# Two graph attention layers on one core: the keys are kept in block order of columns, and VectorE reads two operands through strides

## The reference

```python
def layer0(x, adj):                      # Wq, Wk, Wv, bv, Wo, bo
    q, k = heads(x @ Wq.T), heads(x @ Wk.T)
    v = heads(x @ Wv.T + bv)
    scores = einsum('bqhd,bkhd->bhqk', q, k) * 384**-0.5 + 2 * adj
    scores = where(any(scores != 0, -1), scores, -inf)
    return (softmax(scores) @ v) @ Wo.T + bo

def layer1(x, adj):                      # Wq, bq, Wk, bk, Wv, bv, beta
    q, k, v = heads(x @ Wq + bq), heads(x @ Wk + bk), heads(x @ Wv + bv)
    scores = q @ k.T / sqrt(32) + beta * adj
    scores = where(adj > 0, scores, -9e15)
    return softmax(scores) @ v

x = layernorm(x + layer0(x, adj))        # adj: (128, 128, 128), x: (128, 128, 384)
x = layernorm(x + layer1(x, adj))
```

## Time and profile before

| | before |
|---|---|
| median of 3 runs | 2470.41 us (2469.18 to 2474.57) |
| the profiled execution | 2472.7 us |
| its span, first to last instruction | 2470.9 us |
| TensorE busy | 2158.2 us, 87% |
| VectorE busy | 2100.6 us, 85% |
| ScalarE busy | 1764.0 us, 71% |
| GpSimd busy | 1235.6 us, 50% |
| mean granted TensorE clock | 0.974 |

### The profile page before, as it was taken

The page is one execution under the profiler, slowest core; times in us unless marked ns, Lnnn a source line. Parts: engine busy times, 40 slices in busy tenths (PEclk is TensorE's granted clock), DMA queues, the critical chain, the costliest instruction groups (busy, mean ns, idle before and its releaser), DMA issues.

```text
span 2470.9 us, 84478 instructions
## 1 busy us (share of the span) xinstructions
PE 2158.2 (87%) x23808; PEld 1941.3 (79%) x23808; DVE 2100.6 (85%) x8579; ACT 1764.0 (71%) x7432; POOL 1235.6 (50%) x1932
## 2 busy tenths in 40 slices
PE   5999988898989899889898888898988899889863
PEld 5888888788888788788788888888888888788753
DVE  4788888898888898888898888898888888888864
ACT  5577777777777777677777777777777777677653
POOL 3545555555545555455555555555554555455442
PEclk8999999999999999999999999999999999999976
DMA  4354544544544544454544544544544544454442
GB/s 139 78 131 117 136 127 114 136 124 119 130 121 115 135 126 112 127 131 115 134 126 115 134 125 116 134 124 116 133 124 120 130 124 112 126 131 116 101 116 74
DMA packets 234783, 300.42 MB, mean 122 GB/s; under 512 B 26704, under 2 KB 226384, under 8 KB 234576
## 3 DMA queue, kind: packets, MB, share of 16 engines
q1 hardware_dynamic: 234576, 298.43, 46.6%
HBM read 46.67 MB, written 25.17 MB: 29 GB/s over the span
## 4 chain that ended last, share of the span: by engine, by line
DVE 37%; issue 31%; PE 15%; ACT 11%; DVEq 2%; POOL 2%; ACTq 1%; DMA 1%; SPq 0%; POOLq 0%
DVE neg_s L680 12%; ACT prob L567 8%; DVE abs_max L729 5%; PE s_bank L410 5%; DVE stats L652 3%; DVE neg_max L680 3%; PE r_bank L360 3%; PE r_bank L362 2%; PE r_bank L361 2%; DVE x1T_lo L702 2%; DVE y L744 2%; DVE y L643 2%; PE r_bank L353 1%; DVE flip L696 1%; DVE v L755 1%
## 5 line engine op out<-in xcount | busy, mean ns | idle before, releaser
L567 ACT ACTIVATE prob<-neg_s,neg_max 128x128 f32<-128x128 f32 x3072 | 1186.4, 391 | 391.9 <-DVE neg_max L680 390.0
L680 DVE CUSTOM_DVE_ANT_0 neg_s<-s_bank,bias 128x128 f32<-128x128 f32 x3072 | 673.9, 287 | 184.5 <-PE s_bank L410 115.7
L567 ACT ACTIVATION_READ_ACCUMULATOR prob<-neg_s,neg_max 128x1 f32 x3072 | 587.5, 191 | 0.0
L915 POOL TENSOR_TENSOR prob<-prob,inv_sum 128x512 f32<-128x512 f32 x384 | 388.8, 1041 | 306.8 <-DVE inv_sum L766 306.8
L360 PE MATMUL r_bank<-x1T_hi,w_hi 128*128 128x256 f32 x1152 | 362.7, 315 | 2.7 <-ACT k0T L542 1.4
L907 POOL TENSOR_TENSOR y<-y,x_late 128x384 f32<-128x384 f32 x128 | 127.5, 996 | 474.5 <-DVE y L744 474.5
L360 PE MATMUL r_bank<-xT_hi,w_hi 128*128 128x256 f32 x1152 | 351.2, 305 | 9.5 <-DVE xT_lo L702 9.5
L361 PE MATMUL r_bank<-x1T_lo,w_hi 128*128 128x256 f32 x1152 | 330.1, 287 | 0.0
L362 PE MATMUL r_bank<-x1T_hi,w_lo 128*128 128x256 f32 x1152 | 329.1, 286 | 0.0
L362 PE MATMUL r_bank<-xT_hi,w_lo 128*128 128x256 f32 x1152 | 326.6, 284 | 0.0
L361 PE MATMUL r_bank<-xT_lo,w_hi 128*128 128x256 f32 x1152 | 326.3, 283 | 0.0
(11 more groups left out here) (73 smaller groups left out, 5196.2 us busy)
## 6 DMA issues: line engine op xcount, KB each, us to landing
prob0T<-flip SPq DMA_DIRECT2D x512, 192.0 KB, 3.6
prob1T<-stage SPq DMA_DIRECT2D x512, 192.0 KB, 3.8
x_in<-in_x_dram SPq DMA_DIRECT2D x128, 192.0 KB, 3.3
x_late<-x SPq DMA_DIRECT2D x64, 384.0 KB, 2.6
out_dram<-y SPq DMA_DIRECT2D x128, 192.0 KB, 2.3
adj<-in_adj_dram SPq DMA_DIRECT2D x256, 64.0 KB, 2.3
stage<-in_L_gnn_Wv_dram SPq DMA_DIRECT2D x2, 576.0 KB, 4.2
stage<-in_L_gnn_Wq_dram SPq DMA_DIRECT2D x2, 576.0 KB, 4.9
```

What stands on the lines that cost most here:

```text
L567: act.activation(prob[layer][:, h, :], neg_s[layer][:, h, :], ACT.Exp, bias=neg_max[layer][:, h:h + 1], scale=-1.0, accum_out=row_sum[laye ...
L680: dve.tensor_tensor_reduce(neg_s[layer][:, h, :], s_bank[b][:, (h // HC) * N:(h // HC + 1) * N], bias[layer][q.parity][:, g, :], -1.0, BIG ...
L915: pool.tensor_tensor(prob[0][:, hs, :], prob[0][:, hs, :], inv_sum0[:, hs].unsqueeze(2).to_broadcast([P, HC, N]), ALU.mult).then_inc(probn ...
```

## The change

Nothing is moved from engine to engine, and no instruction is added or taken away; the order on each engine stays. What changes is the addresses that four kinds of instruction walk over.

- `qk_out` copies k as it stands, so that source and destination are both read and written in a row.
- The scores, `neg_s` and `prob` thus have the keys in block order (a j).
- `negate` reads the bias, which still has natural order, with a view that takes elements 32 apart (128 bytes), four of them, and then steps back to the next. Its PSUM input and its output are in a row.
- `flip_probs` reads `prob` with a view that takes, for each head and each j, 32 elements that are 4 apart (16 bytes). What it writes is as before, and so are the DMAs and `probT`.

```diff
@@ qk_out (ScalarE)
                     src = ring(f"g{layer}_{j}")[:, 0:G2]
-                    if j >= C:
-                        src = src.rearrange("p (g a j) -> p g a j", g=2, j=NB)
-                        k_dst = kT[layer][b][:, c, :].rearrange("p (g j a) -> p g a j", g=2, j=NB)
                     if layer == 0:
-                        dst = qT[0][b][:, c, :] if j < C else k_dst
+                        dst = (qT if j < C else kT)[0][b][:, c, :]
                         ins = act.activation(dst, src, ACT.Copy, scale=SCALE0 if j < C else 1.0)
                     elif j < C:
                         ins = act.activation(qT[1][b][:, c, :], src, ACT.Identity, bias=bq1s[:, c:c + 1], scale=SCALE1)
                     else:
-                        ins = act.activation(k_dst, src, ACT.Identity, bias=bqk1[:, 1, c:c + 1])
+                        ins = act.activation(kT[1][b][:, c, :], src, ACT.Identity, bias=bqk1[:, 1, c:c + 1])
                     ins.then_inc(g_out[layer], 1)
@@ negate (VectorE)
                         for h in BANK_HEADS[b]:
-                            dve.tensor_tensor_reduce(neg_s[layer][:, h, :],
-                                                     s_bank[b][:, (h // HC) * N:(h // HC + 1) * N],
-                                                     bias[layer][q.parity][:, g, :], -1.0, BIG, ALU.add, ALU.min,
+                            dve.tensor_tensor_reduce(neg_s[layer][:, h, :].rearrange("p (a j) -> p a j", j=NB),
+                                                     s_bank[b][:, (h // HC) * N:(h // HC + 1) * N
+                                                               ].rearrange("p (a j) -> p a j", j=NB),
+                                                     bias[layer][q.parity][:, g, :].rearrange("p (j a) -> p a j", j=NB), -1.0, BIG, ALU.add, ALU.min,
                                                      neg_max[layer][:, h:h + 1]).then_inc(neg_done[layer], 1)
@@ flip_probs (VectorE)
                     dve.transpose(flip[layer].rearrange("p (j h b) -> p h j b", j=NB, h=H),
-                                  prob[layer][:].rearrange("p h (j a) -> p h j a", j=NB)
+                                  prob[layer][:].rearrange("p h (a j) -> p h j a", j=NB)
                                   ).then_inc(flip_done[layer], 1)
```

## The result

| | before | after |
|---|---|---|
| median | 2471.14 us (2469.18 to 2474.57, 4 runs) | 2961.89 us (2956.95 to 2962.86, 4 runs) |
| ratio | | 1.198, 95% interval 1.1959 to 1.2001 |
| span of the profiled execution | 2470.9 us | 2959.2 us |
| VectorE busy | 2100.6 us, 85% | 2662.3 us, 90% |
| TensorE busy | 2158.2 us, 87% | 2312.8 us, 78% |

The change made the kernel slower by a fifth; 3010 us was forecast, with 2690 to 3420 as the range. In the code after, three lines are gone from `qk_out`, so `negate` is L677, the flip L694, `qk_out` L539 to L543 and `attention_out1` L742.

The account below looks back on a forecast made before the run. VectorE was taken to become the bound: 2100.6 us busy plus 692 us for hopping reads, plus 220 us of remaining waits, gave a 3013 us span, forecast as 3010 us, with 2690 to 3420 us as the range.

Parts of the forecast that it names:

- The slack of a half: In half a round VectorE has 1.4 to 2.2 us of slack; 5.4 us are added, so VectorE sets the period.
- What is taken away: ScalarE's copies of k get 262 and 254 ns shorter, 99 us in all, counted at nothing in the time.
- The price of an element: VectorE's hopping reads in `negate` and flips: 0.88 ns added per element, 692 us together.
- The carry-over by the interval: ScalarE's 1.90 ns per hopping element taken for VectorE too, against 1.02 in a row: an addition of 0.88 ns.
- the one by the addition: ScalarE's surcharge for hopping k writes, 1.02 ns an element, carried over to VectorE's reads.
- The nearest row: ScalarE's k copies, whose destination walks the pattern the bias will be read in: 1.02 ns more an element.
- The waits that stay: Of VectorE's 370 us of idle time 150 go and 220 stay.
- The circle: VectorE reads the ring bank, TensorE transposes x1, then makes scores; VectorE waits 1.2 us, 64 times, 77 us that stay.
- Free reads: Rival: strided reads cost VectorE nothing, leaving only ScalarE's saving; about 2450 us, faster; chance 0.09.
- one pattern alone: Rival: only one of VectorE's 128-byte and 16-byte hops costs, adding 346 us of work; 2720 us; chance 0.14.
- The high price: Rival: VectorE's hopping reads cost 1.5 ns more an element, 1180 us; 3500 us in all; chance 0.09.
- TensorE as the bound: Rival: longer gaps lower TensorE's clock to about 0.7, so its work takes 3000 us; 3250 us in all; chance 0.06.

Follow-up runs that it names:

- experiment 1: The kernel before with only ScalarE's copies of k written in a row, bias and flips unchanged: 2467.35 us, ratio 0.9994.
- experiment 9: The changed kernel, but GpSimd writes the bias in block order so `negate` reads it in a row; flips still hop: 2736.4 us, ratio 1.1065.
- experiments 2 and 3: The kernel before with only `negate`'s bias read in 128-byte hops: 2690.38 us; with only the flips reading `prob` in 16-byte hops: 2759.86 us.

## Why the prediction was right

**The slack of a half.** The step from 1.4 to 2.2 us of slack in a half to "VectorE sets the period" held: the slices stand at nine tenths, and TensorE's share fell to 78% (72% had been forecast, but its slower clock lengthened its busy time by 155 us).

**What is taken away.** 262 and 254 ns a copy, 99 us, counted at nothing: 260 and 256 ns were measured, and 0.9994 (0.9982 to 1.0007) for that part alone. Two things were off and didn't show in the time. The 99 us are the copies' own times; of ScalarE's busy time 60 us went (experiment 1). And in the changed kernel the gain seems to be some 20 us and not nothing (experiment 9).

**The price of an element.** This was the term that was mis-sized: 0.88 ns was taken, 0.73 and 0.75 measured, within the bounds of 0 and 1.5. So VectorE's work grew by 562 us and not 692. The carry-over by the interval (0.88) was nearer than the one by the addition (1.02), but neither holds. Both rest on the copies' own times, in which an overlap with the next instruction is counted; from start to start ScalarE's hop costs some 0.55 ns an element, and VectorE's from start to start 0.73 (0.21 to 0.307 us a head). The nearest row, read by what it costs the engine, lies below VectorE's price and not above it, and would have given some 430 us for VectorE, where 562 were measured. That 0.88 came as near as it did is in part luck.

**The waits that stay.** 220 us were expected and 2959.2 - 2662.3 = 297 measured. The error is in the waits for scores, which were counted at 77 us and come to 125.7 + 29.5 = 155. The circle was counted rightly for the kernel before: 64 waits of over 1 us there, 82 us. After, the 64 are 125 us, 43 more than before. The prediction saw that TensorE's clock goes down behind a long wait, but priced it at the mean of 0.86, 13 us; under the scores behind the longest wait it falls to 0.50, and they take 1.61 us where they took 0.95, which is 42 us in 64 rounds. The other 30 us are mostly short waits, with one of 5.7 us, that were to vanish with the rest and didn't. The terms for ScalarE's copy (22 expected, 21.4) and the last exponential (5 expected, 8.4) were right. The two errors, -130 and +77 us, partly cancel, and that is why 3010 was within 2% of 2962: the mechanism held, and the closeness is largely luck.

**The rivals.** Free reads fell with experiments 2 and 3; one pattern alone fell with the same two. The high price and TensorE as the bound aren't seen. The check that ScalarE's wait for `neg_max` would grow to 900 us was wrong: it grew to 620, because x1's copy waits for TensorE and takes another 214 us more than before (360.3 against 146.2). VectorE's busy share was to be above 90% and is 90.0.

## What to carry to other kernels

To turn the order of data is paid at each element of each instruction that walks across the grain, so count elements times readers: here 98,304 written elements of k (60 us of ScalarE's busy time, all or nearly all hidden) were exchanged for 786,432 read ones (581 us, not hidden). Turn a tile where it is made once, on the engine with room, and not by splitting DMAs on a queue that is half full of issues. A wait that begins when the bound engine finishes something and ends before it can go on is worth most of its length, and a reordering on the other engine can remove it (75 us in the kernel before, 95 in the changed one). The time from one instruction's start to the next one's, and not its duration, says what an instruction costs its engine.

## What the runs showed of the hardware that was not expected

- A hop of 8 bytes costs VectorE's `negate` nothing (287 ns an instruction of 128 elements), nor do runs of two at 16 bytes' distance (286 ns). Single elements at 16 bytes cost the flip 0.75 ns each, and at 128 bytes `negate` 0.73.
- ScalarE's write in hops of 128 bytes, each element alone, lengthens a copy's own time by 1.02 ns an element, but the time to the next instruction's start by only 0.55. In runs of two, 256 bytes apart, a copy takes 393 and 486 ns against 371 and 467.
- GpSimd wrote 128 elements in hops of 16 bytes in 465 and 432 ns against 458 and 405 in a row.
- Behind a wait of 4.06 us TensorE's granted clock was 1.00 for the first half microsecond and fell to 0.50 under the scores that followed.
- SyncE needs a median of 0.59 us to issue a DMA of 48 KB and 0.63 to 0.66 us for one of 192 KB, so the number of issues and not the bytes fills its queue.
